# A local transformer's step, reordered: scores in two parts around the first mixture, the fourth rotation ahead of the maxima, gate and value pairs early

## The reference

```
for each of 6 layers:
    x  = attn_layer(shift_tokens(x)) + x
    x  = ffn_layer(shift_tokens(x)) + x
attn_layer: q, k, v = x @ Wqkv;  q, k = rotary(l2norm(q) * qs), rotary(l2norm(k) * ks)
            each window of 32 queries sees its own and the previous window (64 keys, masked)
            softmax(8 * q k^T) v, then @ Wo
ffn_layer:  xn = layernorm(x) * g + b;  a, gate = split(xn @ W1 + b1)   (341 each)
            (a * gelu(gate)) @ W2 + b2
```

## Time and profile before

| | us |
|---|---|
| median of 3 runs (lowest, highest) | 5454.93 (5452.17, 5469.91) |
| the profiled execution | 5467.54 |
| its span, first to last instruction | 5465.7 |
| TensorE busy (share) | 4689.4 (86%) |
| VectorE busy | 3691.6 (68%) |
| ScalarE busy | 2815.7 (52%) |
| GpSimd busy | 2812.9 (51%) |
| mean granted TensorE clock | 0.935 |

### The profile page before, as it was taken

One profiled execution on the slowest core, in us unless ns is written; L12 is line 12 of the kernel. 1 busy time (PEld: TensorE's weight loads), 2 busy tenths in 40 slices (PEclk: granted clock), 3 DMA queues, 4 the chain that ended last, 5 costly groups with the idle time before them and its releaser, 6 DMA issues. The chain is left out here.

```text
span 5465.7 us, 143416 instructions
## 1 busy us (share of the span) xinstructions
PE 4689.4 (86%) x57103; PEld 3331.9 (61%) x57103; DVE 3691.6 (68%) x8589; ACT 2815.7 (52%) x6208; POOL 2812.9 (51%) x3349
## 2 busy tenths in 40 slices
PE   7699999999999999999999999956284999945896
PEld 3366666666666666666666666644263666623665
DVE  7777777777777777777777777747724656667443
ACT  2266666666666666666665665631023666641342
POOL 4476676767667677766776676711022333311000
PEclk9899999999999999999999999977587999967898
DMA  0211111111111111111111110000211000000002
GB/s 21 71 29 25 25 34 37 25 25 34 29 28 25 33 33 29 25 34 32 28 23 35 25 27 21 17 21 6 68 52 31 2 2 1 1 24 13 26 28 58
DMA packets 312164, 150.62 MB, mean 28 GB/s; under 512 B 146143, under 2 KB 301003, under 8 KB 311243
## 3 DMA queue, kind: packets, MB, share of 16 engines
q1 hardware_dynamic: 309451, 137.20, 10.4%
q0 software_dynamic: 2048, 4.20, 0.3%
HBM read 101.10 MB, written 27.41 MB: 24 GB/s over the span
## 5 line engine op out<-in xcount | busy, mean ns | idle before, releaser
L1436 POOL TENSOR_TENSOR loc_a<-loc_a,loc_b 128x512 f32<-128x512 f32 x768 | 977.7, 1276 | 236.3 <-DVE loc_b L1512 235.6
L1123 PE MATMUL psum<-loc_wqk,loc_xt 128*128 128x512 f32 x1536 | 828.5, 622 | 15.1 <-issue 4.6
L1186 PE MATMUL psum<-loc_m,xn_rows 128*128 128x128 f32 x6144 | 825.2, 278 | 5.0 <-DVE y_rows L1544 3.1
L1307 ACT ACTIVATE loc_sq<-psum 128x512 f32<-128x512 f32 x768 | 455.4, 593 | 685.2 <-PE psum L1123 684.6
L1461 POOL TENSOR_TENSOR loc_a<-loc_a,loc_rn 128x512 f32<-128x512 f32 x768 | 786.0, 1046 | 0.1
L1186 PEld LDWEIGHTS psum<-loc_m,xn_rows 128*128 128x128 f32 x6144 | 755.4, 193 | 47.5 <-issue 44.7
L1508 DVE TENSOR_TENSOR loc_a<-psum,loc_rope 128x512 f32<-128x512 f32 x768 | 523.4, 681 | 336.0 <-ACT loc_sq L1307 323.6
L1468 POOL TENSOR_TENSOR xn_cols<-xn_cols,loc_rec 128x512 f32<-128x512 f32 x384 | 394.0, 1047 | 665.3 <-DVE loc_rec L1539 664.9
L1512 DVE TENSOR_TENSOR loc_b<-psum,loc_rope 128x512 f32<-128x512 f32 x768 | 520.6, 678 | 0.0
L1344 ACT COPY xn_rows<-psum 128x512 f32<-128x512 f32 x768 | 411.9, 588 | 204.0 <-PE psum L1174 200.8
L1516 DVE TENSOR_REDUCE loc_n<-loc_sq 128x8 f32<-128x512 f32 x768 | 516.8, 673 | 0.0
(11 more groups left out here) (370 smaller groups left out, 8551.6 us busy)
## 6 DMA issues: line engine op xcount, KB each, us to landing
loc_x<-loc_shifted SPq DMA_DIRECT2D x192, 256.0 KB, 4.0
loc_shifted<-y_rows SPq DMA_DIRECT2D x144, 64.0 KB
loc_wqk<-in_L_ffn_Wqkv SPq DMA_DIRECT2D x24, 256.0 KB, 3.8
x_rows<-y_rows SPq DMA_DIRECT2D x96, 64.0 KB
x_rows<-y_rows SPq DMA_DIRECT2D x96, 63.5 KB
moe_w<-in_L_ffn_W SPq DMA_DIRECT2D x16, 256.0 KB, 4.7
l3a_qk<-l3a_rot SPq DMA_DIRECT2D x16, 256.0 KB, 2.1
grp_w<-in_L_ffn_W SPq DMA_DIRECT2D x16, 256.0 KB, 4.1
```

Of the source, the lines that this page charges most:

```text
L1123: nc.tensor.matmul(ring("p", i, unit), xt[:, b % 2, t * P:(t + 1) * P], wqk[:, unit * 512:(unit + 1) * 512], start=True, stop=True).then_i ...
L1186: last = nc.tensor.matmul(y_bank[:, 0:P], u[:, i % 2, h // 2, h % 2, :], m[:, h, :], start=(h == 0), stop=(h == HEADS - 1))
L1307: nc.scalar.activation(sq[:, g % 2, :], ring("p", i, unit), ACT.Square).then_inc(sem["squared"], 1)
L1436: nc.gpsimd.tensor_tensor(part, part, b_[:, g % 2, :], ALU.add).then_inc(sem["added"], 1)
```

## The change

Only the order of work within a step changes, on three engines, with the ring's list made to fit.

- TensorE: `scores` becomes `mask_scores` and two halves of four pairs each. They move from between the third and fourth projection to the end of the step: mask, first half, `mix` 0, second half. The three `hidden` pairs move from the end of the step to stand behind `project_out` 0, `project_out` 1 and the last `turn_qk`, ahead of the third projection.
- ScalarE: `exps` moves behind `copy_mixed` 0 and `copy_x`, ahead of `copy_mixed` 1. The three `gelu` move to stand behind the second q copy, and behind each k copy; the table load ahead of them moves along.
- VectorE: the fourth `rotate` comes ahead of `shift_scores`; `gate_hidden` comes behind the second `rotate`.
- The ring: gate and value pairs are listed between the q and the k projections.

```diff
@@ TensorE
-                def scores(i):
-                    b, t = i // TPB, i % TPB
-                    pe.wait_ge(sem["copied"], copied_at["k", i, 1])
+                def mask_scores(i):
+                    t = i % TPB
                     if i >= 1:
                         pe.wait_ge(sem["shifted"], 2 * i)
...
+                def scores(i, pairs):
+                    b, t = i // TPB, i % TPB
+                    if pairs.start == 0:
+                        pe.wait_ge(sem["copied"], copied_at["k", i, 1])
+                    for j in pairs:
...
-                    last.then_inc(sem["scored"], 1)
+                    if pairs.stop == PAIRS:
+                        last.then_inc(sem["scored"], 1)
...
                     if now(4):
                         project_out(n - 4, 0)
+                    if group_at(n, 12) is not None:
+                        hidden(group_at(n, 12), 0)
                     if now(2):
                         turn_qk(n - 2, "k", 0)
                     if now(4):
                         project_out(n - 4, 1)
+                    if group_at(n, 12) is not None:
+                        hidden(group_at(n, 12), 1)
                     if now(2):
                         turn_qk(n - 2, "k", 1)
+                    if group_at(n, 12) is not None:
+                        hidden(group_at(n, 12), 2)
                     if now(0):
-                        project(n, 2)
+                        project(n, K0)
                     if now(3):
                         turn_probs(n - 3, 0)
-                    if now(2):
-                        scores(n - 2)
                     if now(0):
-                        project(n, 3)
+                        project(n, K1)
...
+                    if now(2):
+                        mask_scores(n - 2)
+                        scores(n - 2, range(0, 4))
                     if now(3):
                         mix(n - 3, 0)
-                    if group_at(n, 12) is not None:
-                        hidden(group_at(n, 12), 0)
+                    if now(2):
+                        scores(n - 2, range(4, 8))
                     if n % 2 == 1 and n + 1 < TILES:
                         turn_x((n + 1) // 2)
                     if now(4):
                         project_out(n - 4, 3)
                     if now(3):
                         mix(n - 3, 1)
-                    if group_at(n, 12) is not None:
-                        hidden(group_at(n, 12), 1)
...
-                    if group_at(n, 12) is not None:
-                        hidden(group_at(n, 12), 2)
@@ ScalarE
                     if now(2):
                         copy_turned("q", n - 2, 1)
+                    if group_at(n, 12) is not None:
+                        gelu(group_at(n, 12), 0)
+                    if now(2):
                         copy_turned("k", n - 2, 0)
+                    if group_at(n, 12) is not None:
+                        gelu(group_at(n, 12), 1)
+                    if now(2):
                         copy_turned("k", n - 2, 1)
+                    if group_at(n, 12) is not None:
+                        gelu(group_at(n, 12), 2)
...
-                    if now(2):
-                        exps(n - 2, 0)
-                        exps(n - 2, 1)
-                    if group_at(n, 12) is not None:
-                        nc.scalar.preload_act_table_set("gelu_and_others")
...
                     if n % 2 == 1 and n + 1 < TILES:
                         copy_x((n + 1) // 2)
-                    if group_at(n, 12) is not None:
-                        gelu(group_at(n, 12), 0)
+                    if now(2):
+                        exps(n - 2, 0)
+                        exps(n - 2, 1)
                     if now(3):
                         copy_mixed(n - 3, 1)
@@ VectorE
                     if now(0):
-                        rotate(n, 0)
-                        rotate(n, 1)
+                        rotate(n, Q0)
+                        rotate(n, Q1)
+                    if group_at(n, 12) is not None:
+                        gate_hidden(group_at(n, 12))
                     if group_at(n, 9) is not None:
                         measure_rows(group_at(n, 9))
                     if now(0):
-                        rotate(n, 2)
+                        rotate(n, K0)
+                        rotate(n, K1)
                     if now(2):
                         shift_scores(n - 2)
-                    if now(0):
-                        rotate(n, 3)
-                    if group_at(n, 12) is not None:
-                        gate_hidden(group_at(n, 12))
@@ the ring's list
-                for unit in range(UNITS):
+                for unit in (Q0, Q1):
+                    add_ring(("p", n, unit), "rotated", UNITS * n + unit + 1)
+            if group_at(n, 12) is not None:
...
+            if n < TILES:
+                for unit in (K0, K1):
                     add_ring(("p", n, unit), "rotated", UNITS * n + unit + 1)
```

More of the change, by code:

```diff
@@ L895, in local_transformer_stage @@
     Q, K = 0, 1
+    Q0, Q1, K0, K1 = range(UNITS)
     core.x_in_memory = dram["L0_attn_x"].rearrange("b (t p) c -> p (b t) c", p=P)
@@ L978, in local_transformer_stage @@
             if n < TILES:
-                for unit in range(UNITS):
+                for unit in (Q0, Q1):
+                    add_ring(("p", n, unit), "rotated", UNITS * n + unit + 1)
+            if group_at(n, 12) is not None:
+                for c in range(CH):
+                    add_ring(("gate", group_at(n, 12), c), "gelu_done", CH * group_at(n, 12) + c + 1)
+                    add_ring(("value", group_at(n, 12), c), "h_ready", CH * group_at(n, 12) + c + 1)
+            if n < TILES:
+                for unit in (K0, K1):
                     add_ring(("p", n, unit), "rotated", UNITS * n + unit + 1)
@@ L983, in local_transformer_stage @@
                     add_ring(("w", starts(n, 3), k), "m_copied", 4 * starts(n, 3) + k + 1)
-            if group_at(n, 12) is not None:
-                for c in range(CH):
-                    add_ring(("gate", group_at(n, 12), c), "gelu_done", CH * group_at(n, 12) + c + 1)
-                    add_ring(("value", group_at(n, 12), c), "h_ready", CH * group_at(n, 12) + c + 1)
             if group_at(n, 13) is not None:
@@ L1144, in scores @@
                                              skip_group_check=True)
-                    for j in range(PAIRS):
+                def scores(i, pairs):
[3 more added lines that the diff above has]
+                    for j in pairs:
                         for w in range(WPT):
@@ L1241, in _ @@
                     if now(0):
-                        project(n, 0)
+                        project(n, Q0)
                     if now(2):
@@ L1245, in _ @@
                     if now(0):
-                        project(n, 1)
+                        project(n, Q1)
                     if now(2):
@@ L1369, in gelu @@
                     n, k = INS[c], CH * q + c
+                    if c == 0:
+                        nc.scalar.preload_act_table_set("gelu_and_others")
                     act.wait_ge(sem["gate_done"], k + 1)
@@ L1383, in _ @@
                     if now(0):
-                        square(n, 0)
+                        square(n, Q0)
                     if now(2):
@@ L1389, in _ @@
                     if now(0):
-                        square(n, 1)
+                        square(n, Q1)
                     if now(2):
                         copy_turned("q", n - 2, 1)
+                    if group_at(n, 12) is not None:
+                        gelu(group_at(n, 12), 0)
+                    if now(2):
                         copy_turned("k", n - 2, 0)
+                    if group_at(n, 12) is not None:
+                        gelu(group_at(n, 12), 1)
+                    if now(2):
                         copy_turned("k", n - 2, 1)
+                    if group_at(n, 12) is not None:
+                        gelu(group_at(n, 12), 2)
                     if now(0):
-                        square(n, 2)
+                        square(n, K0)
                     if now(3):
@@ L1399, in _ @@
                     if now(0):
-                        square(n, 3)
+                        square(n, K1)
                     if now(3):
                         copy_turned("p", n - 3, 1)
-                    if now(2):
-                        exps(n - 2, 0)
-                        exps(n - 2, 1)
-                    if group_at(n, 12) is not None:
-                        nc.scalar.preload_act_table_set("gelu_and_others")
                     if group_at(n, 11) is not None:
@@ L1416, in _ @@
                         copy_x((n + 1) // 2)
-                    if group_at(n, 12) is not None:
-                        gelu(group_at(n, 12), 0)
+                    if now(2):
+                        exps(n - 2, 0)
+                        exps(n - 2, 1)
                     if now(3):
                         copy_mixed(n - 3, 1)
```

(4 more changed lines are left out.)

## The result

The changed kernel takes 5481.89 us (median of 9 runs, 5477.3 to 5490.67) against 5461.79 us for the kernel before on the same chips (9 runs, 5451.96 to 5469.91). The ratio is 1.004, 95% interval 1.003 to 1.0051: 20 us slower, where 58 was forecast. The direction is the one forecast, the size about a third of it. The profiled spans are 5487.0 and 5465.7.

A forecast was written before the change was run, and what follows sets the result against it. TensorE's written order and its waits were taken to bound the kernel. Terms +144 + 7 - 36 + 0 - 57 = +58 us gave 5513 us from the median 5454.93, 1.1% slower; range 5415 to 5590.

The forecast's parts named there:

- the wait at the q transposes: TensorE's second q transposes wait for ScalarE's late q copy, 1.08 us, in three steps of four: +144 us.
- the borders: Tile switches on TensorE where score halves meet mask and mixture: 0 net, ends -23 and +23 us.
- the waits inside the scores: TensorE's 54 waits in the score matmuls, 78.0 us, shrink because a mixture stands mid-run: -57 us, bounds 0 and -78.
- S + 5.12: TensorE's own path to the second q transposes, S being the second score half's start; ScalarE's chain takes S + 6.20.
- the plain step's 15.18: Loop check between second q transposes of successive steps: 15.18 us a step, against 14.57 before.
- what is awaited has 1.06 us more: 54 x 1.06: Each of 54 waits in the score run shrinks by the 1.06 us mixture put at its middle: -57 us.
- The early pairs: Moved gate and value pairs: value(0) waits 0.1 to 0.2 us for Q1's rotation, 48 times, +7 us; later pairs nothing.
- What goes: Waits of the second mixture (20.9 us) and turn_x (6.5) vanish, project_out(3)'s slot in step 2 falls to 0.98: -36 us.
- Rival A: Exps do not hold ScalarE up, so TensorE runs through its order and only gains: -93, 5362 us; chance 0.20.
- C: Splitting the score run wins nothing, as each half still runs dry: +115, 5570 us; chance 0.15.
- B: Score waits vanish whole (-78) and new borders cost nothing (-23): +14, 5469 us, no change; chance 0.13.

The follow-up runs named there:

- e4: The kernel before with its score run cut in the middle, after four pairs, by the first probability transposes (0.46 us), nothing else moved: 5398.4 us.
- f5: The kernel before with gate and value pairs early and the score run cut by the first probability transposes: 5399.37 us.
- h1: The kernel before with its score run cut by the first probability transposes after seven pairs instead of four: 5413.55 us.
- h2: The kernel before with its score run cut by the first probability transposes after two pairs instead of four: 5395.22 us.
- f1: The kernel before with only the gate and value pairs, gelus, gating and ring list early as in the change: 5437.22 us.
- e2: The changed kernel with the score run whole again and put ahead of the first mixture: 5441.02 us.
- e1: The changed kernel with the score run whole again and put behind the first mixture: 5469.1 us.

## Why the prediction was right and where it was wrong

The mechanism held, and so did the direction; what failed are sizes. Three terms of the sum were off: the wait at the q transposes (+144 forecast, +109 measured), the borders, which were put at nothing and cost about 26, and the waits inside the scores (-57, measured -80). The first two nearly cancel, the third stays. The slots (start to next start) below are medians over the steps of the table above, summed over a group of four steps and multiplied by 48.

| term | forecast | measured |
|---|---|---|
| slot ahead of the second q transposes (4.02 to 6.29 us a group) | +144 | +109 |
| score run with its borders (1.39 to 1.56 a step) | part of 0 | +33 |
| probability transposes and the projection between them (7.84 to 7.69 a group) | part of 0 | -7 |
| old waits around the second mixture and turn_x (6.14 to 5.22 a group) | -36 | -44 |
| gate and value pairs and the rest of step 0 | +7 | -1 |
| waits inside the scores (means against medians) | -57 | -80 |
| sum | +58 | +10 |

Measured were +20. The remaining 10 us are not in these steps: the table leaves out each layer's first ones. Of them 4 us are known, the wait of the weight products (6.8 to 10.7 us), whose copies stand behind the exps.

**The deciding term, right in kind, too large: +144 forecast, 109 by slots, 106 by idle time.** ScalarE's chain came within 0.07 us (6.13 against 6.20). What failed is the step "S + 5.12", TensorE's own path. The half run takes 0.79 and not 0.70 (2428.78 to 2429.57), project_out(3) behind it 1.09 and not 0.98: I had taken half of a whole run's slot and the slot of a project_out that followed transposes, both without the cost of the border that the change itself makes. From S the path is 0.79 + 1.09 + 2.46 (2430.66 to 2433.12) + 0.98 (that projection's slot where nothing waits) = 5.32, so the wait by slots is 6.13 - 5.32 = 0.81 against 1.08. This is no gain of 0.2 us: TensorE works in that time instead of waiting, and the q transposes come at S + 6.13 either way.

**Borders: 0 forecast, about +26 measured.** The term was taken as the middle of its bounds, not from a row. The scores in two parts cost 0.17 a step, and the 0.12 that was to go with the transposes ahead of the mask went in steps 1 and 2 only (1.96 to 1.85); steps 0 and 3 show 1.98 and 2.01. With the wait's +109 this makes +135 where +144 was forecast, so these two errors nearly cancel, and the plain step's 15.18 came out right (15.21).

**The waits inside the scores: -57 forecast, -70 by the named waits, -80 by means against medians.** This is the largest error that no other term makes good, 23 of the 38 us between forecast and result. Start to start, the pauses above 0.3 us inside the run add up to 91.6 us before and 13.3 after, -78, which bears out the larger figure. The sign held. The step that failed is "what is awaited has 1.06 us more: 54 x 1.06", a wait shortened by the length of the pause put in: in e4 a pause of 0.46 us takes 76 of the 78 us, where that rule gives 25.

**The early pairs: +7 for value(0), measured 6.5.** Booking nothing for the rest was right in the sum (f5), but I had not seen that a wait of the second mixture moves from step 1 to step 0.

**What goes: -36 forecast, -44 measured.** The second mixture's 20.9 us and turn_x's 6.5 are gone. The slot of project_out(3) in step 2 fell from 1.34 to 1.09, not to 0.98.

Rival A (no wait) is refuted by the 138 waits, and C (the split wins nothing) fell. B (no change) names +14, which is nearer to the measured +20 than the forecast is. Part of that is luck: its score term of -78 was right, but it kept the wait at 144 and took 23 us off for borders that cost about 26.

## What to carry to other kernels

When one engine's order is the bound, follow the hand-over with the least room (here the single transpose bank, 0.15 us) through every in-order queue that the change touches: an instruction that waits for a late result, put ahead of copies that were ready, costs its whole delay. Time both sides of such a race from slots that already contain the new borders, and book the borders in the sum too, since work that fills a wait takes nothing off the time. And before reordering for waits that name no engine, cut the densest run of instructions alone: that one edit was worth 66 us, three times what the whole reordering cost.

## What the runs showed of the hardware

The pauses inside the scores come at one place of TensorE's own instruction count. I counted all records of its queue in the packed traces: matmuls, weight loads and semaphore instructions. In the 13 traces there are 380 pauses above 0.3 us between two score records, and 374 of them end at a record whose number is 194 modulo 256. TensorE has 117595 records in the kernel before, 459 times 256, and one queue brings nearly as many transfers, 461 of 16 KB each:

```profile
q8 instruction: 461, 7.55, 0.6%
```

In the kernel before, pauses are there only where that place lies 160 or more instructions into the run of 272: in 5 of 19 runs where it is between 160 and 191, 15 of 23 up to 223, 18 of 24 up to 255, all 18 in the last 16, none of 126 below 160. They end 2.2 to 2.9 us after the start of the last transfer on the instruction queue. The Trainium skill (Runtime: NRT & Kernel Launch, Instruction fetch mechanics) gives blocks of 256 instructions, each fetched while the one before runs: the traces agree on the 256. They disagree on "mostly hidden": a run of 272 instructions in 1.6 us lost 78.0 us in 54 waits. h1 and h2 fit it. In h1 30 pauses are left in the long piece, all at places 160 to 239 and about as often as before (5 of 23, 14 of 23, 11 of 16): a cut helps where it lies inside the passage of the block that would run out.

What stays open is the size. The same whole run, at the same kind of place in the count, waits 78.0 us (before), 59.6 (f1), 52.1 (e2) and 20.8 (e1) in all. These kernels differ in what TensorE does in the microseconds ahead of the run; which part of that decides was not tried. The speed of passage alone does not: in the kernel before, the 256 records ahead of a pause took from 1.4 to 7.2 us (median 2.9), and the awaited transfer began 0.5 to 7.1 us after TensorE had passed the 194 before. What makes a transfer begin late is not shown.

The fastest kernels of the study are e4 and h2, the kernel before with its score run cut in two and nothing else changed: 5398.4 and 5395.22 us, 1.2% faster than before, and 84 to 87 us faster than the changed kernel.
